# Layer 1 feed-forward of a four-layer gated block: another fp4 rounding, weights rounded in layer 0's attention, one phase in place of six

## What is computed

```
_GRID = [0.0, 0.5, 1.0, 1.5, 2.0, 3.0, 4.0, 6.0]
_MID  = [0.25, 0.75, 1.25, 1.75, 2.5, 3.5, 5.0]
def fp4_quant_dequant(x):                 # blocks of 16 along the last dim
    scale = maximum(max(abs(xb)) / 6.0, 1e-12)
    xn = xb / scale
    idx = searchsorted(_MID, abs(xn))
    return _GRID[idx] * sign(xn) * scale
def fp4_linear(x, w): return fp4(x) @ fp4(w).T
h = layernorm(x)
y = fp4_linear(silu(fp4_linear(h, w_gate)) * fp4_linear(h, w_up), w_down)
x = x + tanh(g_ffn[1]) * y                # w_gate, w_up: 352x128, w_down: 128x352
```

## Time and profile before

| | us |
|---|---|
| median of 3 runs (5976.93 to 5980.03) | 5979.7 |
| the profiled execution's own time | 5979.15 |
| its span, first to last instruction | 5977.4 |
| PE busy | 5196.6 (87%) |
| DVE busy | 4557.3 (76%) |
| ACT busy | 3034.3 (51%) |

### The profile page before, as it was taken

One profiled execution on the slowest core, in us unless ns is written; L12 is line 12 of the kernel. 1 busy time (PEld: TensorE's weight loads), 2 busy tenths in 40 slices (PEclk: granted clock), 3 DMA queues, 4 the chain that ended last, 5 costly groups with the idle time before them and its releaser, 6 DMA issues. The chain is left out here.

```text
span 5977.4 us, 75371 instructions
## 1 busy us (share of the span) xinstructions
PE 5196.6 (87%) x27320; PEld 1979.9 (33%) x27320; DVE 4557.3 (76%) x5110; ACT 3034.3 (51%) x5833; POOL 1443.0 (24%) x1136
## 2 busy tenths in 40 slices
PE   8936999999999999999992389999998589999997
PEld 4413444444444444444441122222222312222222
DVE  6346867787777767787767789999994589999993
ACT  2212444444444444444440048888885158888884
POOL 0013545454454545454450200000000200000000
PEclk9968999999999999999995679999997689999996
DMA  0023324232233324232200211111110221111100
GB/s 28 1 90 89 86 68 112 53 108 47 83 78 85 88 65 115 53 105 50 50 22 4 80 29 25 20 20 25 20 21 4 79 33 20 21 24 20 25 16 5
DMA packets 164055, 293.81 MB, mean 49 GB/s; under 512 B 26492, under 2 KB 103752, under 8 KB 160616
## 3 DMA queue, kind: packets, MB, share of 16 engines
q1 hardware_dynamic: 111560, 163.29, 10.3%
q10 hardware_dynamic: 52128, 125.71, 9.5%
HBM read 178.92 MB, written 109.89 MB: 48 GB/s over the span
## 5 line engine op out<-in xcount | busy, mean ns | idle before, releaser
L1587 DVE TENSOR_REDUCE a_mx<-ps 128x1 f32<-128x1024 f32 x1536 | 1820.1, 1220 | 151.6 <-PE ps L1467 129.3
L1554 ACT ACTIVATE a_prob<-ps 128x512 f32<-128x512 f32 (+1 forms) x3264 | 1705.3, 601 | 427.0 <-PE ps L1455 422.3
L1152 POOL TENSOR_TENSOR tot_p<-tot_p,prob 128x512 f32<-128x512 f32 (+1 forms) x896 | 1265.1, 1412 | 834.3 <-ACT prob L1040 767.6
L1074 DVE TENSOR_REDUCE mx<-ps 128x1 f32<-128x1024 f32 x896 | 1052.5, 1216 | 427.3 <-PE ps L860 427.3
L1040 ACT ACTIVATE prob<-ps 128x512 f32<-128x512 f32 (+1 forms) x1888 | 980.0, 606 | 671.3 <-PE ps L885 570.9
L1467 PE MATMUL ps<-a_K,a_Q 51*128 51x512 bf16 (+1 forms) x3328 | 1068.4, 385 | 49.8 <-DMA a_Q<-q_stack_dram 30.4
L1455 PE MATMUL ps<-a_Q,a_K 51*128 51x512 bf16 (+1 forms) x3264 | 1003.7, 389 | 82.8 <-ACT a_prob L1554 76.7
L1491 PE MATMUL ps<-a_prob,a_V 128*9 128x512 f32 x6528 | 953.9, 609 | 10.9 <-ACT a_acc L1538 10.9
L896 PE MATMUL ps<-prob,V 128*64 128x512 f32 (+1 forms) x3776 | 954.8, 615 | 0.0
L884 PE MATMUL ps<-QA,KA 128*128 128x512 f32 (+1 forms) x1888 | 854.7, 453 | 73.5 <-ACT prob L1040 72.7
L1097 DVE TENSOR_TENSOR tot_d<-tot_d,prob 128x512 f32<-128x512 f32 x928 | 831.2, 896 | 75.7 <-ACT prob L1040 24.5
(11 more groups left out here) (348 smaller groups left out, 3348.6 us busy)
## 6 DMA issues: line engine op xcount, KB each, us to landing
a_K<-k_stack_dram SPq DMA_DIRECT2D x64, 600.4 KB, 5.9
k_hi_dram<-hi_s SPq DMA_DIRECT2D x112, 256.0 KB, 2.0
k_lo_dram<-lo_s SPq DMA_DIRECT2D x112, 256.0 KB, 2.1
KA<-k_hi_dram ACTq DMA_DIRECT2D x64, 384.0 KB, 4.3
KA<-k_lo_dram ACTq DMA_DIRECT2D x64, 384.0 KB, 5.5
KB<-k_hi_dram ACTq DMA_DIRECT2D x64, 384.0 KB, 6.5
k_bf_dram<-bf_s SPq DMA_DIRECT2D x112, 128.0 KB, 2.6
KM<-k_bf_dram ACTq DMA_DIRECT2D x32, 448.0 KB, 6.6
```

What stands on the lines that cost most here:

```text
L1074: nc.vector.tensor_reduce(mx[:, u % 2, j, i % FULL:i % FULL + 1], c.banks(slot(n), 2), AX.X, ALU.max).then_inc(released, 1)
L1152: nc.gpsimd.tensor_tensor(tot_p[0:r, u % 2, :], tot_p[0:r, u % 2, :], p, ALU.add).then_inc(totalled_p, 1)
L1554: nc.scalar.activation(prob[0:r, batch % 2, t % BATCH, :], c.banks(n % 3)[0:r, :], ACT.Exp, scale=SCALE).then_inc(exped, 1)
L1587: nc.vector.tensor_reduce(mx[:, u % 2, j, i % FULL:i % FULL + 1], c.banks(slot(step), 2), AX.X, ALU.max).then_inc(maxed, 1)
```

## The change

- `fp4_round` is written anew with 16 DVE instructions: three of one element per block, five `tensor_scalar` over all elements, eight others over all elements. The size |x/scale| is one instruction. Sizes up to 2 are rounded to whole halves by adding and subtracting 1.5 * 2^23, the larger by three comparisons; the sign is put back at the end.
- The weights are rounded in layer 0's attention phase. POOL clears a buffer, SP loads the weights into it, DVE rounds one weight (384 columns, padded) in its second half behind tile 10, 18 and 26 each, and SP stores each to HBM.
- `l1_ffn` is one phase. SP loads the rounded weights; PE transposes them; ACT copies them out, ahead of its square root. DVE computes the norm and the rounding of h directly. y is copied out in halves by DVE and ACT. Two tiles' banks rotate in gate and up. The product is rounded in two halves of 1408 columns; PE and ACT transpose, copy and project the first while DVE rounds the second.

```diff
@@ l0_attention
+        F4 = F1_TILES * D
+        fp4_w, fp4_q = sb("fp4_w", [P, 3, F4]), sb("fp4_q", [P, 3, F4])
+        FP4_AT = (10, 18, 26)
...
+            @block.sync
+            def _(sp):
+                sp.wait_ge(fp4_clear, 1)
...
+                    sp.dma_start(tiles[:, 0:F1_TILES - 1, :],
+                                 fp4_in[i][0:(F1_TILES - 1) * P, :].rearrange("(t p) d -> p t d", p=P)
+                                 ).then_inc(fp4_in_done, 16)
...
+                for i in range(3):
+                    sp.wait_ge(fp4_rounded, i + 1)
+                    sp.dma_start(fp4_out[i], fp4_q[:, i, :].rearrange("p (t d) -> p t d", d=D)).then_inc(fp4_stored, 16)
+                sp.wait_ge(fp4_stored, 48)
+            @block.gpsimd
+            def _(pool):
+                nc.gpsimd.memset(fp4_w[:], 0.0).then_inc(fp4_clear, 1)
...
                         if f == 1 and t == FIN_AT:
                             finish(0)
+                        if f == 1 and t in FP4_AT:
+                            i = FP4_AT.index(t)
+                            dve.wait_ge(fp4_in_done, 80)
+                            fp4_round(nc, link, fp4_w[:, i, :], fp4_q[:, i, :], fp4_size[:], fp4_step[:], fp4_inv[:],
+                                      fp4_top[:])
+                            nc.vector.engine_nop().then_inc(fp4_rounded, 1)
@@ fp4_round
-    link(v.tensor_tensor(in_blocks(mag), in_blocks(src), over_block(inv), ALU.mult))
-    link(v.tensor_scalar(dst, mag, MID[6], 2.0, ALU.is_gt, ALU.mult))
-    for m in (MID[5], MID[4]):
-        link(v.scalar_tensor_tensor(out=dst, in0=mag, scalar=m, in1=dst, op0=ALU.is_gt, op1=ALU.add))
...
-    for m in MID[:4]:
-        link(v.scalar_tensor_tensor(out=dst, in0=mag, scalar=m, in1=dst, op0=ALU.is_gt, op1=ALU.add))
+    link(v.tensor_tensor(in_blocks(step), in_blocks(src), over_block(inv), ALU.mult))
+    link(v.scalar_tensor_tensor(out=size, in0=step, scalar=-1.0, in1=step, op0=ALU.mult, op1=ALU.max))
+    link(v.tensor_scalar(dst, size, 2.0, 2.0 - 2.0 ** -22, ALU.min, ALU.mult))
+    link(v.tensor_scalar(dst, dst, NEAREST, None, ALU.add))
+    link(v.tensor_scalar(dst, dst, NEAREST, None, ALU.subtract))
+    link(v.tensor_scalar(step, size, 5.0, 2.0, ALU.is_gt, ALU.mult))
+    for middle in (3.5, 2.5):
+        link(v.scalar_tensor_tensor(out=step, in0=size, scalar=middle, in1=step, op0=ALU.is_gt, op1=ALU.add))
+    link(v.scalar_tensor_tensor(out=dst, in0=step, scalar=2.0, in1=dst, op0=ALU.mult, op1=ALU.add))
     link(v.tensor_scalar(top, top, 0.5, None, ALU.mult))
     link(v.tensor_tensor(in_blocks(dst), in_blocks(dst), over_block(top), ALU.mult))
+    link(v.tensor_scalar(step, src, 0.0, 2.0, ALU.is_ge, ALU.mult))
+    link(v.scalar_tensor_tensor(out=dst, in0=step, scalar=-1.0, in1=dst, op0=ALU.add, op1=ALU.mult))
@@ l1_ffn, now one phase
+            @block.sync
+                for dst, src in zip((wg, wu, wd), rounded):
+                    sp.dma_start(dst[:], src).then_inc(weights_in, 16)
...
+            @block.tensor
+                    if t >= 2:
+                        pe.wait_ge(silu_done, t - 1)
+                        pe.wait_ge(up_done, t - 1)
...
+                for f in range(HALVES):
+                    pe.wait_ge(hid_ready, f + 1)
...
+            @block.vector
+                for f in range(HALVES):
+                    some = slice(HQ * f, HQ * (f + 1))
+                    dve.wait_ge(up_done, HQ * (f + 1))
+                    fp4_round(nc, link, flat(up[:, some, :]), flat(hid_q[:, some, :]), size[:], step[:], inv[:], top[:])
+                    nc.vector.engine_nop().then_inc(hid_ready, 1)
+                for f in range(HALVES):
+                    some = slice(HQ * f, HQ * (f + 1))
+                    dve.wait_ge(projected, f + 1)
+                    link(nc.vector.scalar_tensor_tensor(
+                        out=c.x[:, some, :], in0=c.banks(1 + f).rearrange("p (t d) -> p t d", t=HQ), scalar=c.gf[:, 1:2],
+                        in1=c.x[:, some, :], op0=ALU.mult, op1=ALU.add))
```

More of the change, by code:

```diff
@@ L200, in _, with l0_attention @@
             add_to_x(nc, link, c, c.y[:], gate)
[L205 removed]
+def l0_attention(c, w, x_in, ctx_in, gx_in, gf_in, fp4_in, fp4_out):
     nc = c.nc
@@ L1662, in _, with fp4_round @@
                 last.then_inc(projected, 1)
-MID = [0.25, 0.75, 1.25, 1.75, 2.5, 3.5, 5.0]
 BLK = 16
-def fp4_round(nc, link, src, dst, mag, inv, top):
+NEAREST = 1.5 * 2.0 ** 23
+F1 = 352
+F1_TILES = -(-F1 // P)
+def fp4_round(nc, link, src, dst, size, step, inv, top):
     r, n = src.shape[0], src.shape[1] // BLK
@@ L1694, in fp4_round @@
-    for _ in range(2):
-        link(v.scalar_tensor_tensor(out=dst, in0=mag, scalar=-MID[6], in1=dst, op0=ALU.is_lt, op1=ALU.add))
-    link(v.tensor_scalar(dst, dst, 2.0, None, ALU.mult))
-    for m in MID[:4]:
-        link(v.scalar_tensor_tensor(out=dst, in0=mag, scalar=-m, in1=dst, op0=ALU.is_lt, op1=ALU.add))
-    link(v.tensor_scalar(dst, dst, -1.0, None, ALU.mult))
-    for m in MID[:4]:
-        link(v.scalar_tensor_tensor(out=dst, in0=mag, scalar=m, in1=dst, op0=ALU.is_gt, op1=ALU.add))
+    link(v.tensor_tensor(in_blocks(step), in_blocks(src), over_block(inv), ALU.mult))
@@ L1750, in l1_ffn @@
-        with phase(nc, "chain", "gate_ready", "up_ready", "silu_done", "up_done") as (
-                block, chain, gate_ready, up_ready, silu_done, up_done):
-            @block.tensor
-            def _(pe):
-                for t in range(QT):
-                    if t >= 4:
-                        pe.wait_ge(silu_done, t - 3)
-                        pe.wait_ge(up_done, t - 3)
-                    lhs = c.hT[:, t * P:(t + 1) * P]
-                    nc.tensor.matmul(c.banks(t % 4)[:, 0:F], lhs, gT[:], start=True, stop=True).then_inc(gate_ready, 1)
-                    nc.tensor.matmul(c.banks(4 + t % 4)[:, 0:F], lhs, uT[:], start=True, stop=True).then_inc(up_ready, 1)
-            @block.scalar
-            def _(act):
-                for t in range(QT):
-                    act.wait_ge(gate_ready, t + 1)
-                    nc.scalar.activation(hid[:, t, :], c.banks(t % 4)[:, 0:F], ACT.Silu).then_inc(silu_done, 1)
-            @block.vector
-            def _(dve):
-                link = Chain(dve, chain)
-                for t in range(QT):
-                    dve.wait_ge(up_ready, t + 1)
-                    dve.wait_ge(silu_done, t + 1)
-                    nc.vector.tensor_tensor(up[:, t, :], hid[:, t, :], c.banks(4 + t % 4)[:, 0:F], ALU.mult
-                                            ).then_inc(up_done, 1)
-                dve.wait_ge(up_done, QT)
-                fp4_round(nc, link, flat(up[:]), flat(hid_q[:]), scratch[:], inv[:], top[:])
@@ new lines, in _ @@
+                dve.wait_ge(std_ready, 1)
+                link(nc.vector.reciprocal(rstd, rstd))
+                link(nc.vector.tensor_tensor(tmp, rstd, rstd, ALU.mult))
+                link(nc.vector.tensor_tensor(tmp, tmp, var, ALU.mult))
+                link(nc.vector.tensor_scalar(tmp, tmp, -0.5, 1.5, ALU.mult, ALU.add))
+                link(nc.vector.tensor_tensor(rstd, rstd, tmp, ALU.mult))
+                link(nc.vector.tensor_tensor(c.h[:], c.h[:], rstd.unsqueeze(2).to_broadcast(wide), ALU.mult))
@@ new lines, in _ @@
+                fp4_round(nc, link, flat(c.h[:]), flat(c.y[:]), size[:, 0:N], step[:, 0:N], inv[:, 0:N // BLK],
+                          top[:, 0:N // BLK])
+                nc.vector.engine_nop().then_inc(y_ready, 1)
+                dve.wait_ge(y_turned, 1)
+                nc.vector.tensor_copy(c.hT[:, 0:CH], c.banks(0)).then_inc(hT_ready, 1)
+                for f in range(HALVES):
+                    for t in range(HQ * f, HQ * (f + 1)):
+                        dve.wait_ge(up_ready, t + 1)
+                        dve.wait_ge(silu_done, t + 1)
+                        nc.vector.tensor_tensor(up[:, t, :], hid[:, t, :], c.banks(4 + t % 2)[:, 0:F1], ALU.mult
+                                                ).then_inc(up_done, 1)
@@ L2081 @@
                 for n, dtype in ((n + "_hi", FP32), (n + "_lo", FP32), (n + "_bf", BF16))]
+    scratch += [nc.dram_tensor(f"fp4_{n}_dram", (P, F1_TILES, D), _mybir.dt.float32, kind="Internal").ap()
+                for n in ("gate", "up", "down")]
     build(nc, args, out, scratch)
```

164 lines of the change are left out of this document (99 added, 65 removed).

## The result

The changed kernel took 5885.5 us (median of 4 runs, 5881.9 to 5888.9), the kernel before beside it 5979.6 (4 runs, 5976.9 to 5980.0). The ratio is 0.9843, with a 95% interval of 0.9826 to 0.9860. The prediction was 5884.0 with a range of 5876 to 5894. The profiled execution of the changed kernel took 5887.5 us with a span of 5885.6.

A forecast was written before the change was run, and what follows sets the result against it. DVE was taken to bound layer 1's feed-forward (busy 145.6 of 183.4 us) and PE layer 0's attention. The terms summed to 95.7 us, taken from the profiled 5979.15: 5883.5, or 5884.0 for the median, range 5876 to 5894.

The forecast's parts named there:

- The weights' rounding: Layer 1's feed-forward: the stretch from 3174.55 to 3220.21 goes from the block, 45.7 us gained there.
- The square root: Layer 1's norm: the root waits on ACT behind four weight copies, 2.5 us lost, bounds nothing and 6.
- y to gate: From y to the first gate product in layer 1: 8.85 us becomes 2.8, 6.0 gained.
- Gate and up: Layer 1's gate and up products: 12.1 us in both kernels, change zero, bounds -1 and +1.5.
- The product's rounding: Layer 1's rounding of the gate and up product: 59.95 us becomes 38.3 in two halves, 21.6 gained.
- The tail: Layer 1, last rounding to last add: 14.6 us becomes 8.5, with 4.0 for 24 product passes; 6.1 gained.
- the dearer hand-overs: Rival: ACT's table switches in layer 1 cost 2.6 us more and late weights 3, 5889.6 us; chance 0.09.
- full passes for `tensor_scalar`: Rival: the rounding's five `tensor_scalar` run as full passes, 10.0 us more in all, 5894.0 us; chance 0.03.
- uncovered layer 0: Rival: layer 0's attention hides none of the three weight roundings, 22.4 us more, 5906.4 us; chance 0.05.
- The slower one: Rival: a stall in layer 0 lowers PE's clock and it stays down, 5995.8 us; chance 0.01.
- "nothing" in layer 0: Layer 0's attention: each 7.5 us rounding costs nothing, as DVE may be away 13.2 us and is level five tiles later.
- My sign of being wrong: Among signs of error: any stage outside the two changes altering its length by more than 2 us.

The follow-up runs named there:

- the rounding alone: The kernel before with only fp4_round replaced by the new form, weights rounded where they were: 5927.6 us, ratio 0.9916.
- the weights at home: The kernel after, with weights loaded raw and rounded by DVE in layer 1's feed-forward, square root ahead of the weight copies: 5906.2 us, ratio 0.9877.
- the run with the root first: The kernel after, with ACT taking the square root ahead of its copies of the turned weights: 5877.0 us, block 87.6 us.
- the second profile: The kernel after, unaltered, run and profiled again: median 5888.7 us, ratio 0.9857, block 88.3 us.

## Why the prediction held, step by step

The forecast's mechanism is what happened. The medians are 94.2 us apart and the blocks of the two profiles 93.3, and the runs divide the latter, each part good to 1 or 2 us: the new rounding 50.5, the weights moved away 22.8, the new form of the block 22.7 (the block of the rounding alone, 133.0, less that of the weights at home, 110.3, where the root came first), and 2.6 lost by the root that waits. Of the 22.7, 7.3 come from the weights' rounding itself, which took 29.7 us in five pieces with copies and takes 22.4 in three without; about 15 are the one phase with its hand-overs and halves.

1. *The load phase*, 4.8: DVE starts 0.95 behind the add. Right.
2. *The end of the norm*, 4.1: no gap. Right.
3. *The weights' rounding*, 45.7 off the block: right, and at no cost in layer 0 (96.59 us in both).
4. *The square root*, 2.5 lost: 2.86 less 0.28 is 2.6. The whole loss goes with the order of ACT's work, as the run with the root first shows. The weights reached PE at 3165.4, in line with the 4 us behind the barrier that the old load phase had shown.
5. *The rounding of h*, 14.8: 14.7.
6. *y to gate*, 2.8: 2.84. The Trainium skill (ScalarE: Activation LUTs, "What ACT_TABLE_LOAD costs") has a drain of 1.38 us with each table change. The load starts 0.02 us behind the copy, and the square root runs 0.01 behind the load's 1.28 (3168.10 to 3169.39). The sum by that rule was 92.9, and 93.3 was measured, but not for its reason: the hand-over has the length forecast without a drain, and what is missing from 95.7 is in items 7 and 9. At the second place, Silu starts 0.39 us behind the load's end and waits for PE, so a drain of 1.38 has no room there either (3189.37 to 3191.05). On the drain the measurement decides.
7. *Gate and up*, nothing: 0.96 us more in this pair of profiles, 0.84 of it on the path, since the rounding of the first half starts before DVE's last product ends. The granted clock rose 5.5 us after the first gate product, and 3.7 after it in the profile before. That is scatter and not the change: the old code took 12.1 and 13.1 us in its two profiles, the new 11.7 to 13.0 in the five of the same block. So "nothing" is right within what two profiles of one kernel differ by. The products of PE were on the path at either level (10.3 us at the high clock throughout).
8. *The product's rounding*, 38.3: 38.2, a full pass 1.66 with its link, a half 0.93. The three small instructions come to the 1.2 allowed, though not as the prediction had it from the earlier trace rows, at 0.17 to 0.3 each: the reciprocal of 88 elements takes 0.70 and the other two 0.2.
9. *The tail*, 8.5: 9.95, and 9.4 at the least in five profiles of this block. The mis-sized term. I took 4.0 us for the 24 passes, between 2.8 and 5.6; they took 5.49, the low end of the clock, and 4.92 in the second profile. Of the rest, 3.6 was allowed before the passes and 3.6 passed (3240.66 to 3244.26).

The two misses, 0.84 and 1.45, make 2.3 of the 2.4 between 95.7 and 93.3, and both are PE's clock behind idle time. By the second profile's block of 88.3 the gain is 95.2. So the total came out closer than its terms deserve: 0.5 to 2.4 us of miss in the block is about what two profiles of one kernel differ by, and the medians, 1.5 us from the forecast, carry a scatter of several us from outside the block. That the forecast is 1.5 off and not 5 is luck; that the parts add up is not.

Of the rivals, the dearer hand-overs, full passes for `tensor_scalar` and uncovered layer 0 are each excluded by a row above (2.84 us; 0.89 for 1408 columns; 96.59 us). The slower one needed a clock that stays down; it comes back some 10 us after a stall, which is longer than the "few us" of the prediction, and layer 0 had no stall. The reasoning behind "nothing" in layer 0 held in both its conditions: 7.4 us against the 13.2, and the arrears gone 11.5 us after DVE left (7.4 / (1 - 0.78/2.18)) against a spacing of 17.4. (15.3 - 1.3 - 0.7 is 13.3 and three times 7.5 is 22.5; the prediction has each 0.1 lower, which changes nothing.)

My sign of being wrong, that a stage outside the two changes its length by more than 2 us, did appear: layer 1's attention was 7.7 us longer in the profile after, and the first part of layer 0 4.3 shorter. The same kernel's second profile had its block start 7.6 us earlier, so this is not the change. I set that bound without having looked at how two profiles of one kernel differ.

## What to carry to other kernels

Work can be hidden beside a ring of buffers if two things hold. The longest absence is less than the ring's depth in time, less the engine's own work on a tile (13.2 us here), plus what the engine that sets the time has ahead (3.7 here). And the time between two absences is enough to work off the arrears, absence / (1 - own time per tile / tile time): 14.9 us of rounding every 17.4 us cost 6.6, every 26.2 us nothing. When a stage is cut in two so that one part hides behind the other, cut it so that the covered part just ends when the cover does: what is left is short, and PE comes to it at the high clock (a tail of 3.75 us in place of 9.4 to 9.95). And where TensorE has short work behind long idle time on the path, price it at the low clock; turns of the identity matrix ahead of it gave 5.5 to 7.3 us of a block of 88 to 90.

## What the runs showed of the hardware that I had not expected

A single idle time of 1.9 us in PE was followed by about 10 us at a granted clock of 0.50, in a stretch where PE was otherwise never idle; the low clock cost more than twice the stall. The clock's return from the low level was not the same each time: gate and up, with the same work ahead of them, took 11.7 to 13.0 us in nine profiles, according to when it rose (3.1 us after the first gate product in the second profile of after, 5.5 in the first).

The place where the block begins, with the same program ahead of it, lay between 3151.9 and 3164.3 us in the profiles of the kernel after and of those that change the block (two of them also the rounding in layer 0, which is hidden there). Where these 12 us of scatter come from was not followed to its end; in the pair compared, before and after, the difference lay in single steps of layer 1's attention, most steps being equal within 0.1 us. They are larger than seven of the nine terms of the prediction, which only the rows inside the block could show.
